# Attention over 2304 tokens on one core: another place for the turn, for the shift rows and for the norm chain, and another order of loads

## What is computed

```python
g = group_norm(x, groups=32)                       # 16 channels per group
q, k, v = Wq g, Wk g, Wv g                          # 8 heads of 64
attn = softmax(q^T k, axis=-1)                      # no scaling, 2304 x 2304 per head
out = x + gamma * (attn v) + Wsc g
```

## Time and profile before

| | us |
|---|---|
| median of three runs (3330.66 to 3332.46) | 3330.93 |
| profiled execution | 3337.42 |
| its span | 3335.7 |
| PE busy | 3174.5 (95%) |
| POOL busy | 2801.2 (84%) |
| DVE busy | 2109.5 (63%) |
| ACT busy | 2078.5 (62%) |
| granted TensorE clock, mean | 0.991 |

### The profile page before, as it was taken

One profiled execution on the slowest core, in us unless ns is written; L12 is line 12 of the kernel. 1 busy time (PEld: TensorE's weight loads), 2 busy tenths in 40 slices (PEclk: granted clock), 3 DMA queues, 4 the chain that ended last, 5 costly groups with the idle time before them and its releaser, 6 DMA issues.

```text
span 3335.7 us, 119917 instructions
## 1 busy us (share of the span) xinstructions
PE 3174.5 (95%) x52880; PEld 2174.1 (65%) x52880; DVE 2109.5 (63%) x3568; ACT 2078.5 (62%) x3443; POOL 2801.2 (84%) x2104
## 2 busy tenths in 40 slices
PE   4899999999999999999999999999999999999998
PEld 3576666666667666576666666666676666767666
DVE  6666666666666666566666666656666666666674
ACT  3465656766565655776656565676656656566665
POOL 1588978989898888999889887799988989888889
PEclk7999999999999999999999999999999999999999
DMA  3010000100001000110001100001000000000000
GB/s 122 13 40 26 12 22 25 37 29 12 26 31 35 23 14 21 33 33 26 12 26 31 45 12 12 26 30 45 11 17 12 17 12 16 12 17 12 16 17 14
DMA packets 53030, 82.66 MB, mean 25 GB/s; under 512 B 4384, under 2 KB 50464, under 8 KB 52512
## 3 DMA queue, kind: packets, MB, share of 16 engines
q1 hardware_dynamic: 52512, 74.99, 7.0%
HBM read 56.10 MB, written 18.87 MB: 22 GB/s over the span
## 4 chain that ended last, share of the span: by engine, by line
PE 77%; DVE 11%; POOL 7%; issue 3%; ACT 2%; DMA 0%; SPq 0%; DVEq 0%; POOLq 0%
PE SL L397 21%; PE PJ L331 13%; PE MX L372 10%; PE OB L415 9%; PE OB L418 7%; PE OB L417 7%; PE PJ L328 6%; POOL PLO L822 6%; DVE mx L630 4%; DVE mx L635 2%; DVE xr L617 2%; PE PJ L356 1%; PE SL L392 1%; DVE QK L593 1%; POOL DF L803 1%
## 5 line engine op out<-in xcount | busy, mean ns | idle before, releaser
L822 POOL TENSOR_TENSOR PLO<-PE 128x768 f16<-128x768 f32 x1728 | 2493.9, 1466 | 470.0 <-ACT PE L508 470.0
L508 ACT ACTIVATE PE<-SL 128x768 f32<-128x768 f32 x1728 | 1311.0, 815 | 40.6 <-PE SL L397 40.6
L415 PEld LDWEIGHTS OB<-V,PE 128*128 128x128 bf16 x10368 | 952.2, 99 | 263.9 <-POOL PLO L822 142.0
L415 PE MATMUL OB<-V,PE 128*128 128x65 f16 x10368 | 1076.3, 194 | 25.1 <-POOL PLO L822 22.9
L417 PE MATMUL OB<-V,PE 128*128 128x64 f16 x10368 | 1067.2, 193 | 0.0
L418 PE MATMUL OB<-V,PLO 128*128 128x65 f16 x10368 | 1066.3, 196 | 0.0
L627 DVE TENSOR_REDUCE mx<-MX 128x1 f32<-128x384 f32 x864 | 481.0, 557 | 920.5 <-PE MX L372 919.9
L516 ACT ACTIVATE MXC<-MX 128x384 f32<-128x384 f32 x864 | 424.9, 492 | 992.5 <-PE MX L372 991.7
L397 PE MATMUL SL<-QK 64*128 64x384 f16 x10368 | 1002.5, 323 | 0.0
L417 PEld LDWEIGHTS OB<-V,PE 128*128 128x128 bf16 x10368 | 966.8, 97 | 1.0
L418 PEld LDWEIGHTS OB<-V,PLO 128*128 128x128 f16 x10368 | 966.5, 98 | 0.0
(11 more groups left out here) (85 smaller groups left out, 1371.3 us busy)
## 6 DMA issues: line engine op xcount, KB each, us to landing
gx<-x SPq DMA_DIRECT2D x36, 768.0 KB, 4.5
xr<-x SPq DMA_DIRECT2D x96, 192.0 KB, 2.4
out<-xr SPq DMA_DIRECT2D x96, 192.0 KB, 1.9
X<-x SPq DMA_DIRECT2D x6, 768.0 KB, 10.9
QK<-wk SPq DMA_DIRECT2D x1, 1024.0 KB, 8.7
QK<-wq SPq DMA_DIRECT2D x1, 1024.0 KB, 13.1
QK<-wv SPq DMA_DIRECT2D x1, 1024.0 KB, 13.3
QK<-wsc SPq DMA_DIRECT2D x1, 1024.0 KB, 14.7
```

The source lines that it names most:

```text
L415: pe.matmul(acc, upper, v[:, D:V1], start=k == 0 and h == 0 and i == 0, stop=False, skip_group_check=True)
L508: act.activation(PE32[:, s % PB, :].rearrange("p (h n) -> p h n", h=2), SL[s % 2][:, :, 0:CH], ACT.Exp, scale=1.0 / SS).then_inc(s_exp, 1)
L822: nc.gpsimd.tensor_tensor(PLO[:, s % PB, :], PE32[:, s % PB, :], PE32[:, s % PB, :].bitcast(BF16)[:, 1:4 * CH:2], ALU.subtract).then_inc(s ...
```

## The change

1. `slot_unit`: step 0 has no projection; `sc` lies in steps 1 and 2, the next block's units in steps 3 to 8. A unit is issued in sixths of its matmuls (`project(u, lo, hi)` up to 6): the first half in odd steps, the second half in even ones as a sixth and, behind the shift rows and the group sum where there are any, two sixths. `turn` stands behind both `weigh` of step 0, and its product on VectorE in step 1. `AHEAD` spreads the six key units over c0, c1 and c2, two in each.
2. The shift rows no longer use PJ but the columns 384 to 511 of three score banks, which are free (`shift_bank`), and the group sums four columns of the fourth (`ROOT`). They wait for the last exponential of the chunk. With own semaphores they are out of the order of PJ.
3. Of the norm chain VectorE keeps the reading of the sums and the reciprocal; nine 128 x 4 operations go to GpSimd, three in step 1 of c2, six in step 4 of c3.
4. Of the four low halves per chunk in block 2 two go to VectorE, in steps 7 and 8.
5. In the last block VectorE makes the first 192 of the 768 columns of each split (`SHARE`), GpSimd the rest.
6. The opening loads the six pieces of x and then the four weights; the weights are transposed in other banks (`WB`), one between two steps of the scaling; GpSimd makes three of the six low halves; and each of the eleven units beside maximum tiles is issued in two halves, one behind each tile.

```diff
@@ slot_unit, done_at
-    if m == DS - 1:
+    if m == 0:
         return None
-    if m < 2:
+    if m < 3:
         return ("sc", n)
...
-    kind, part = AHEAD[3 * c + m // 2 - 1]
+    kind, part = AHEAD[3 * c + (m - 3) // 2]
...
+def done_at(M):
+    if M < 0 or M % DS == 0 or M % DS % 2 == 1:
+        return None
+    return slot_unit(M // DS, M % DS)
@@ banks
+        def shift_bank(n):
+            if n == 0:
+                return OB[:, 0:CH].rearrange("p (i n) -> p i n", i=QT)
+            return SLS[:, 0:QT, CH:CH + P]
+        ROOT = SLS[:, 3, CH:CH + CT]
@@ sync
             for c in range(NCH):
                 sp.dma_start(first[:, c, :, :], rows[:, :, c * CH:(c + 1) * CH]).then_inc(s_x0[c], 16)
-                if c in (1, 3, 4, 5):
-                    w = (1, 3, 4, 5).index(c)
...
+            for w in range(4):
+                src = (wk, wq, wv, wsc)[w].rearrange("(t p) c -> p t c", p=P)
+                sp.dma_start(wnat[:, w, :, :], src).then_inc(s_wld[w], 16)
@@ tensor
+            def root(b, part):
+                if b:
+                    pe.wait_ge(s_exp, (b - 1) * PAIRS * NCH * MT + (NCH + 2 + part) * MT)
+                pe.wait_ge(s_gv, 3 * b + 1 + part)
+                pe.matmul(ROOT, gmat[:, :], gn_var if part else mv[:, :, 0], start=True, stop=True).then_inc(s_rt, 1)
             def shift_rows(n):
-                u = ("c", n)
-                left(same_bank_before(u))
+                if n:
+                    pe.wait_ge(s_exp, n * MT)
                 pe.wait_ge(s_cc, 3 * n + 3)
...
+            weights(0)
+            root(0, 0)
+            root(0, 1)
+            weights(1)
+            for kind, c in FIRST:
+                if kind == "k" and c in (2, 4):
+                    weights(c // 2 + 1)
+                project((kind, 0, c))
...
                 top(2 * i)
+                project((kind, 0, c), 0, 3)
                 top(2 * i + 1)
+                project((kind, 0, c), 3, 6)
...
+                    if s:
+                        weigh(s - 2)
+                        weigh(s - 1)
                     if m == 0 and n >= 2:
                         turn(n - 2)
-                    if s:
-                        weigh(s - 2)
+                    u = slot_unit(n, m)
+                    if u:
+                        project(u, *((0, 3) if m % 2 else (3, 4)))
                     if m == DS - 1 and n + 1 < CHUNKS:
                         shift_rows(n + 1)
-                    if s:
-                        weigh(s - 1)
...
+                    if u and m % 2 == 0:
+                        project(u, 4, 6)
@@ vector
+            def split(s):
+                dve.wait_ge(s_exp, s + 1)
+                nc.vector.tensor_tensor(PLO[:, s % PB, 0:SHARE], PE32[:, s % PB, 0:SHARE],
+                                        PE32[:, s % PB, 0:SHARE].bitcast(BF16)[:, 1:2 * SHARE:2],
+                                        ALU.subtract).then_inc(s_restd, 1)
...
                     if U < TOPS:
                         top(U)
-                    if m == DS - 1 and last:
-                        leave(last)
-                    if m == 0 and n >= 2:
-                        leave(("f", n - 2))
+                    if s > LAST:
+                        split(s - 1)
                     if U < TOPS:
                         top_other(U)
...
+                    if m == 1 and n >= 2:
+                        leave(("f", n - 2))
...
                     if U < TOPS:
                         top(U + 1)
+                    if s >= LAST:
+                        split(s)
+                    if norm_part(n, m, 5) and norm_part(n, m, 5)[2] >= CT // 2:
+                        b, c, t = norm_part(n, m, 5)
+                        dve.wait_ge(s_gh, NCH + CT * (NCH * b + c) + t + 1)
+                        one = nc.vector.tensor_tensor(
+                            X[:, (b + 1) % 2, 1, t, c * CH:(c + 1) * CH], gx[:, t, :],
+                            X[:, (b + 1) % 2, 0, t, c * CH:(c + 1) * CH], ALU.subtract)
@@ gpsimd
+            def root_scale(b):
+                pool.wait_ge(s_gr, b + 1)
+                link(nc.gpsimd.tensor_tensor(gn_a, gn_r, gn_r, ALU.mult))
+                link(nc.gpsimd.tensor_tensor(gn_b, gn_a, gn_ve, ALU.mult))
+                link(nc.gpsimd.tensor_scalar(gn_a, gn_b, -0.5, 1.5, ALU.mult, ALU.add))
+                link(nc.gpsimd.tensor_tensor(gn_rstd, gn_r, gn_a, ALU.mult))
+                link(nc.gpsimd.tensor_tensor(gn_b, gn_mean, gn_rstd, ALU.mult))
+                nc.gpsimd.tensor_scalar(gn_bias, gn_b, -1.0, None, ALU.mult).then_inc(s_rstd, 1)
...
+            for c in range(0, NCH, 2):
+                pool.wait_ge(s_gh, c + 1)
+                nc.gpsimd.tensor_tensor(X[:, 0, 1, :, c * CH:(c + 1) * CH], first[:, c, :, :],
+                                        X[:, 0, 0, :, c * CH:(c + 1) * CH], ALU.subtract).then_inc(s_gl[0], 1)
```

More of the change, by code:

```diff
@@ L35 @@
 BLOCKS = BATCH * PAIRS
+SHARE = 192
 CHUNKS = BLOCKS * NCH
@@ L75, in units @@
 def units():
[L77 to L79 removed]
+    out = [(kind, 0, c) for kind, c in FIRST + BESIDE]
     for n in range(CHUNKS):
[L81 to L89 removed]
+        if n >= 2:
+            out.append(("f", n - 2))
+        out += [done_at(n * DS + m) for m in range(DS) if done_at(n * DS + m)]
     out += [("f", CHUNKS - 2), ("f", CHUNKS - 1)]
@@ L211, in build @@
         s_gh = sem("s_gh")
-        s_gl = sem("s_gl")
-        s_gno = sem("s_gno")
+        s_gl = [sem(f"s_gl{i}") for i in range(2)]
+        s_gno = [sem(f"s_gno{i}") for i in range(2)]
         s_gv = sem("s_gv")
@@ L274, in _ @@
                     elif b:
-                        sp.wait_ge(s_gno, NCH * b)
+                        for e in range(2):
+                            sp.wait_ge(s_gno[e], NCH * b)
                     load_piece(b + 1, c)
@@ L278, in _ @@
                     if c:
-                        sp.wait_ge(s_gno, NCH * b + c)
+                        for e in range(2):
+                            sp.wait_ge(s_gno[e], NCH * b + c)
                     else:
@@ L322, in project @@
                     work = [(0, *x) for x in terms]
-                half = len(work) // 2
-                for i, wp, p, t in work[lo * half:hi * half]:
+                sixth = len(work) // 6
+                for i, wp, p, t in work[lo * sixth:hi * sixth]:
                     edge = dict(start=(wp, p, t) == terms[0], stop=(wp, p, t) == terms[-1])
@@ L381, in score @@
                 else:
-                    for u in UNITS[OPENING - 6:OPENING - 1]:
+                    for u in UNITS[OPENING - 5:OPENING - 1]:
                         left(u)
                 if k == 0:
-                    pe.wait_ge(s_pja, LEFT["c", n])
+                    pe.wait_ge(s_cr, n + 1)
                     pe.wait_ge(s_dk, KCOUNT["k", g, NCH - 1])
+                if k == 1 and n and root_unit(n - 1, DS - 1):
+                    b, part = root_unit(n - 1, DS - 1)[1:]
+                    pe.wait_ge(s_rtf, 2 * b + part + 1)
                 q = slice(c * CH, (c + 1) * CH)
@@ L423, in _, with weights @@
             pe.wait_ge(s_const, 3)
-            for w in range(4):
+            def weights(w):
                 pe.wait_ge(s_wld[w], 16)
@@ L549, in _ @@
                         top_copy(U)
-                    before = slot_unit(n, m - 1) if m and m % 2 == 0 else None
+                    before = done_at(n * DS + m - 1)
                     if before:
@@ L722, in scale, with weights @@
+            def weights(w):
+                for t in range(CT):
+                    dve.wait_ge(s_wh, w * CT + t + 1)
+                    nc.vector.scalar_tensor_tensor(
+                        out=WT[:, w, 1, t, :], in0=WB[t][:, :], scalar=WS, in1=WT[:, w, 0, t, :],
+                        op0=ALU.mult, op1=ALU.subtract).then_inc(s_wf, 1)
             def scale(c):
@@ L743, in _ @@
                 leave((kind, 0, c))
-            for i, (kind, c) in enumerate(BESIDE):
-                leave((kind, 0, c))
+            for i in range(len(BESIDE)):
                 top(2 * i)
                 top_other(2 * i)
+                if i:
+                    leave((BESIDE[i - 1][0], 0, BESIDE[i - 1][1]))
                 top(2 * i + 1)
@@ L751, in _ @@
                     shift_parts(0)
+            leave((BESIDE[-1][0], 0, BESIDE[-1][1]))
             for n in range(CHUNKS):
@@ L791, in _ @@
                             root_var(b)
+            split(STEPS - 1)
             leave(("f", CHUNKS - 2))
```

287 lines of the change are left out of this document (151 added, 136 removed).

## The result

| | us |
|---|---|
| median before, 4 runs (3330.66 to 3332.46) | 3331.14 |
| median after, 4 runs (3240.65 to 3242.82) | 3242.37 |
| ratio, 95% interval | 0.9732 (0.9720 to 0.9744) |
| predicted, range | 3264 (3215 to 3304) |
| profiled execution after, its span | 3242.41, 3240.7 |

A forecast was written before the change was run, and what follows sets the result against it. TensorE's matmul stream was taken as the bound, GpSimd as the second; 3330.5 - 49.5 - 18 + 7 + 20 - 26 = 3264 us, 2.0% faster, range 3215 to 3304.

The forecast's parts named there:

- Base: Start of the sum: profiled 3337.42 us less 6.9 us for an accidental VectorE stall in the last block, 3330.5.
- A: Chunk steps: turn beside no projection, shift rows in score banks, projections in sixths; -3.3 us per block, -49.5 in 15 blocks.
- Both waits for VectorE: TensorE's waits in step 0 and at the end of step 8, worth 0.35 and 0.43 us, were to go.
- B: Statistics chain moved to GpSimd: 3.6 us per batch instead of 9.0, -18 us in all.
- late by 1.5: Norm chain: GpSimd's tiny operations, 1.2 and 2.4 us against 0.7 slack per step, delay splits by 1.5 us.
- C: Half of the normalised low parts moved to VectorE: 9.1 us lateness instead of 6.8 per batch, +7 for three batches.
- D: Last block, splits shared with VectorE: 32.2 us per chunk against 27.9, over 4.8 chunks, +20 us.
- E: Opening: earlier loads, statistics and scaling, shorter rounds; chunk 0 starts near 90.5 us, -26 us.
- (1): Rival for C and D: exclusion costs little, waits fall into slack; D -8, C -12, total 3217 us; chance 0.15.
- (2): Rival for A: GpSimd's backlog takes half of it, leaving -25, total 3288 us; chance 0.17.
- (3): Rival for C and D: VectorE loses at each boundary between GpSimd instructions, total 3347 us; chance 0.06.
- (4): Rival for A: the waits only move to step 1, A is 0, total 3313 us; chance 0.05.

The follow-up runs named there:

- experiment 1: Changed kernel with VectorE's share of the last block's splits undone, GpSimd making them whole: 3233.96 us.
- experiment 4: Changed kernel with the keys' units spread over the block, at most one per chunk after the first: 3230.66 us.
- Experiment 7: Changed kernel with the norm chain's small operations of batches 1 to 3 put back on VectorE: 3259.46 us.
- experiment 5: Changed kernel with all four low halves of the next batch's x back on GpSimd: 3243.08 us.
- experiment 3: Changed kernel with the shift rows' parts issued ahead of VectorE's moved low half at step 7: 3231.64 us.
- experiment 8: Changed kernel with all six lower halves of x in the opening on VectorE, none on GpSimd: 3238.68 us.
- experiment 2: Changed kernel with VectorE's last-block share replaced by a maximum with one SBUF operand, those low halves not computed: 3230.28 us.
- experiment 12: Changed kernel without shares, with shift parts first, keys spread, all opening lower halves and all four norm low halves on VectorE: 3225.85 us.

## Why the prediction was nearly right

**Base.** Taking 6.9 us off the profiled execution was right: the last block without shares takes 175.25 us in experiment 1 against 182.6 - 6.9 = 175.7.

**A, -53.1 for -49.5.** The starts of the first maximum product of steps 0 to 2 of a chunk are 1679.35, 1682.65 and 1686.25: step 0 takes 3.31 us (3.22 by hand), a step 3.60 as said. Both waits for VectorE are gone; in step 1 its wide reduction ends 3.2 us after the start. GpSimd is next late, as worked out, by 0.06 in step 7, 0.14 in step 8 and 0.44 behind it (0.13, 0.08 and 0.55 by hand), only that the last shows in step 1 and not in step 0. The plain block was said to take 195.9 and takes 195.67; experiment 4 confirms that the keys' backlog on GpSimd is the cause of what is left, while the two waits were not put back by any run. That the block came within 0.2 us is partly luck: by the text's own figures it is 6 x 32.18 + 12 x 0.03 = 193.4 us before the backlog, not 194.0, and step 0 is 0.09 longer than by hand, 0.5 per block. The slip in the addition and the one in step 0 cancel.

**B, -22.3 for -18.** The term mis-sized is the tiny operation, estimated at 0.4 us with hand-over: it takes 0.24 to 0.27. Three and six of them cost 0.71 and 1.61 us instead of 1.2 and 2.4, inside the slack of the step's splits, so the "late by 1.5" did not come. Experiment 7 shows that the chain's place on GpSimd is worth 15.3 us of the 22.3; the rest, which came with the other parts, was not taken apart. Of the 1.6 us that remain per batch 1.4 are in c3 (34.21 against 32.84 in a plain block), where ScalarE has its table loads, as the text said:

```profile
1185.08 1.28 ACT L619 ACT_TABLE_LOAD   x1
...
1186.98 1.28 ACT L542 ACT_TABLE_LOAD   x1
```

The copy of the maximum tile waits for the first, the exponentials for the second, and steps 1 and 2 of c3 take 4.74 and 4.18 us. No run takes the loads away, so their share is read and not shown.

**C, +2.6 for +7.** Of the lateness in block 2, 9.1 us by the text, 7.7 came. But the forecast charged it to the moved low halves, and experiment 5 shows that it was not theirs: with all four back on GpSimd the block is as long (203.52). For c3 to c5 the working holds nearly instant by instant: low half asked for 2.70 us into step 7 (2.78 by hand), done at 3.91 (3.95), shift's operation done at 5.28 (5.42), 1.05 lost (1.2). For c0 to c2 the 1.8 was too high: they lose 1.2 to 1.5. The text had added VectorE's wait to GpSimd's backlog; but experiment 3, which takes VectorE's wait away, leaves c1 at 34.38 us against 34.39: there the backlog alone decides.

**D, +6.8 for +20: the largest error.** The mechanism was right (steps of 3.28 between others of 3.05, a share ending when a split ends), its count was wrong. The text gave 32.2 us per chunk against 27.9, with 4.05 in step 1, 3.8 in step 3 and 4.3 in step 7. Measured, from step 0: 3.84, 3.60, 3.61, 3.05, 3.29, 3.06, 3.37, 2.97, 3.41, in sum 30.2 against 27.97. Where a projection or another operation lengthens the step, the share's wait lies in its slack; I had added it on top. So a chunk lost 2.2 us and not 4.3. And the loss lasts four chunks, not 4.8: the fifth loses 0.7 us, and the last does not "stay" but gains 2.5, because in its last steps, without reductions, a step takes 2.44 us with shares and 2.85 without (starts of the exponentials).

The Trainium skill ("SBUF — State Buffer", section "Who interferes with whom") says that a VectorE instruction with two SBUF inputs excludes a GpSimd one that reads SBUF, and that a reduction never does on this chip. The traces agree with both: 628 ns against 344.

**E, -21.4 for -26.** Loads, statistics (18.09, 18.2 by hand), start of scaling (26.21, 26.1) and rounds (2.84, 2.8) came as worked out. The first maximum product came at 63.58 instead of 59.1, and one failing term is GpSimd's lower half of 1536 columns: the line through its operations of 384 and 768 columns gave 2.5 us, and it takes 3.10. Three of them explain at most 1.8 of the 4.5 us; the rest lies in how the by-hand working let scalings, weight splits and lower halves overlap, and the text doesn't show that step by step. With VectorE making all six instead, chunk 0 starts at 90.50 in experiment 8 and at 92.4 to 92.5 in the other two runs; that the first equals the predicted 90.5 is chance, for it is another kernel, and the text's own 59.1 + 30.8 is 89.9.

**Rivals.** (1), exclusion that falls into slack, gave D -8 and C -12. It is refuted as a whole, for experiment 1 shows D at +7.2, and even shares without any wait would have won only 175.7 - 171.54 = 4.2 us (experiment 2). But its mechanism is what made D 6.8 instead of 20. (2), -25 for A, would have been 197.5 us per plain block, not 195.67. (3), VectorE losing at each boundary, would have given steps of 5.6 us; no step of the changed kernel has it, but its mechanism, a VectorE operation that comes second at such a boundary, is real: experiment 12 has steps of 5.60 by it. (4) is refuted by steps 1 of 3.60; the 4.04 behind chunks with two keys' units are GpSimd's backlog.

## What to carry to other kernels

Moving a small two-operand instruction between VectorE and GpSimd doesn't share their work: each stops the other, and a 0.16 us operation of VectorE costs up to a whole GpSimd instruction, so tiny chains belong on the engine whose long instructions would block them. When such an operation is unavoidable on VectorE, don't put two behind each other, and let nothing that TensorE waits for stand behind it; which engine goes first between two GpSimd instructions can't be counted on. To say what a part of a change is worth, undo it alone: block 2 of a batch came to lie 7.7 us over a plain block instead of 6.8, and undoing part C, to which the difference had been charged, gave none of it back. When costs of one mechanism are added up over the steps of a loop, check each step's slack first, since a wait counts only where the step has none.

## What was unexpected of the hardware

- A scaling of 128x384 with a single tile operand (0.47 us alone) took up to 2.68 us while GpSimd's subtraction ran; a reduction with one operand never did (0.33 to 0.35 us in all 108 of experiment 2). The Trainium skill, in the same section, counts the scaling's kind of instruction among those that can take both port pairs and then exclude GpSimd, and the trace agrees.
- GpSimd's subtraction of 1536 columns took 3.10 us, 768 took 1.47, 576 took 1.15, 384 to a 16-bit result 0.92; its operations of 4 columns about 0.27 from start to start.
- The same opening, in eight executions, started chunk 0 between 92.92 and 95.68 us, while a plain block repeats within 0.1 us. An effect of 2 us is read from its own stretch, not from the span.
